# mLSTM stage: the gate products of the layer input between the two tiles' head products, and the next turn ahead of turning back

## The reference, cut to what matters

```
xm, z = split(x @ W_up)                 # 288 features each
xs    = silu(conv(xm)); q, k = xs @ Wq, xs @ Wk;  v = xm @ Wv
ig    = [q,k,v] @ Wi + bi;  fg = [q,k,v] @ Wf + bf
log_D = cumsum(log_sigmoid(fg)) differences + ig, causal
C     = (q k^T / sqrt(36)) * exp(log_D - max)
h     = (C / normalizer) @ v;  h = layernorm per head
out   = ((h + skip * xs) * silu(z)) @ W_down;  x = x + out
```

## Time and profile before

| | us |
|---|---|
| median of 3 runs | 2554.04 (2553.14 to 2554.78) |
| the profiled execution, its own time | 2551.11 |
| its span, first to last instruction | 2549.3 |
| TensorE busy | 2162.4 (85% of the span) |
| VectorE busy | 1468.7 (58%) |
| ScalarE busy | 894.0 (35%) |
| GpSimd busy | 833.8 (33%) |
| mean granted clock of TensorE | 0.879 |
| nine turns of the mLSTM stage, from the scores of turn 0 to those of turn 9 (93.85 to 353.59) | 259.74 |

### The profile page before, as it was taken

The page is one execution under the profiler, slowest core; times in us unless marked ns, Lnnn a source line. Parts: engine busy times, 40 slices in busy tenths (PEclk is TensorE's granted clock), DMA queues, the critical chain, the costliest instruction groups (busy, mean ns, idle before and its releaser), DMA issues. The chain is left out here.

```text
span 2549.3 us, 46768 instructions
## 1 busy us (share of the span) xinstructions
PE 2162.4 (85%) x17513; PEld 1876.4 (74%) x17513; DVE 1468.7 (58%) x3846; ACT 894.0 (35%) x1929; POOL 833.8 (33%) x799
## 2 busy tenths in 40 slices
PE   8999995689789857996899979998999996663598
PEld 7778873477678756995677668887999996552497
DVE  1666776656667764533999863332444336777434
ACT  0444446522244413333556531111111113676111
POOL 0111015700011063554656530330333331472446
PEclk9988995799899958997999989998999998655599
DMA  9900000090000054551000014013656652000353
GB/s 272 192 1 1 1 1 20 3 228 2 2 2 2 2 186 153 177 184 51 11 11 11 1 38 183 28 38 104 231 207 215 216 178 63 1 1 0 122 171 122
DMA packets 118115, 218.72 MB, mean 86 GB/s; under 512 B 14539, under 2 KB 90262, under 8 KB 111106
## 3 DMA queue, kind: packets, MB, share of 16 engines
q1 hardware_dynamic: 106978, 195.05, 24.8%
q0 software_dynamic: 10912, 20.67, 2.5%
HBM read 164.55 MB, written 51.11 MB: 85 GB/s over the span
## 5 line engine op out<-in xcount | busy, mean ns | idle before, releaser
L2745 ACT ACTIVATE bl_swiglu_sg<-psum 128x384 f32<-128x384 f32 x102 | 50.0, 490 | 303.5 <-PE psum L2692 303.5
L2681 PE MATMUL psum<-bl_swiglu_xt,bl_swiglu_w 128*128 128x128 f32 x1224 | 147.5, 278 | 2.2 <-DVE bl_swiglu_hid L2798 1.6
L2681 PEld LDWEIGHTS psum<-bl_swiglu_xt,bl_swiglu_w 128*128 128x128 f32 x1224 | 145.5, 195 | 3.0 <-issue 3.0
L2643 POOL COPY bl_swiglu_w<-ahead_w2swiglu_w 128x1152 f32 x51 | 58.2, 1143 | 272.5 <-PE psum L2703 213.9
L2772 DVE COPY bl_swiglu_xt<-psum 128x256 f32<-128x256 f32 x51 | 21.7, 425 | 198.1 <-PE psum L2662 198.1
L2159 POOL DMA_INDIRECT rows_in<-tower_h,tower_spots x66 | 65.1, 986 | 173.4 <-DVE tower_spots L3096 140.0
L2757 ACT ACTIVATE bl_gelu_hid<-psum,bl_gelu_w 128x128 f32<-128x128 f32 x258 | 71.1, 376 | 111.6 <-POOL bl_gelu_w L2643 108.4
L2703 PE MATMUL psum<-bl_swiglu_w,bl_swiglu_hid 128*128 128x192 f32 x612 | 107.9, 326 | 0.0
L2703 PEld LDWEIGHTS psum<-bl_swiglu_w,bl_swiglu_hid 128*128 128x128 f32 x612 | 98.3, 190 | 0.1
L3028 ACT ACTIVATE shared_sg<-psum 128x512 f32<-128x512 f32 x54 | 32.2, 597 | 187.8 <-PE psum L2965 187.8
L2958 PE MATMUL psum<-tower_xT,shared_w 128*128 128x256 f32 x432 | 96.4, 380 | 0.6 <-ACT tower_xT L3022 0.6
(11 more groups left out here) (694 smaller groups left out, 6028.2 us busy)
## 6 DMA issues: line engine op xcount, KB each, us to landing
bl_swiglu_w<-in_swiglu_w SPq DMA_DIRECT2D x51, 1152.0 KB, 5.1
bl_gelu_w<-in_gelu_w SPq DMA_DIRECT2D x43, 576.0 KB, 4.4
bl_relu_w<-in_relu_w SPq DMA_DIRECT2D x25, 576.0 KB, 4.3
rows_in<-tower_zeros SPq DMA_DIRECT2D x1, 14065.0 KB, 62.9
rows_in<-tower_zeros SPq DMA_DIRECT2D x1, 13968.0 KB, 61.0
ahead_w2swiglu_w<-in_swiglu_w SPq DMA_DIRECT2D x1, 9216.0 KB
tok_x<-in_x SPq DMA_DIRECT2D x11, 648.0 KB, 12.6
ahead_w2gelu_w<-in_gelu_w SPq DMA_DIRECT2D x1, 5400.0 KB
```

Of the source, the lines that this page charges most:

```text
L2643: pool.tensor_copy(w2[:, n % DEEP], w2all[:, e, :].rearrange("p e n -> p (e n)")).then_inc(s_w2, 1)
L2681: pe.matmul(up_tile(n, j, i, side), w[:, o:o + 128], xt[:, n % 2, side, :], start=(i == 0), stop=False, skip_group_check=True)
L2745: act.activation(sg[:, j], bank_pair(n, j)[:, 0, 0:3 * BLOCK].rearrange("p (i n) -> p i n", i=3), ACT.Silu).then_inc(s_silu, 1)
```

## The change

Three things. The two gate products of pair p + 1 (one over 128 rows, one over 64) leave `project` and become `gates_of_input`, which `attend(p)` calls behind the eight head products of the first tile. They now open the sum in bank 4 (`start`), and the first product of the queries no longer does. `p_o` is signalled by the last head product as before. In front of the turns the two are called right before `queries(0)`. And `turn(p + 2)` stands ahead of `turn_back(p)`.

```diff
                     for m in range(4):
                         for k in range(2):
                             pe.wait_ge(c_xs, MC * p + k + 1)
-                            pe.matmul(out(m), w[:, k, m * 128:(m + 1) * 128], xs[:, k, :], start=(m % 2 == 0 and k == 0), stop=False,
-                                      skip_group_check=True)
-                        if gate and m == 0:
-                            pe.matmul(out(0), wgx[:, 0, :], hT[:, p % 2, 0, :], start=False, stop=False, skip_group_check=True)
-                            pe.matmul(out(0), wgx[64:128, 1, :], hT[64:128, p % 2, 1, :], start=False, stop=False, skip_group_check=True)
+                            pe.matmul(out(m), w[:, k, m * 128:(m + 1) * 128], xs[:, k, :],
+                                      start=(m % 2 == 0 and k == 0 and not (gate and m == 0)), stop=False, skip_group_check=True)
...
+                def gates_of_input(p, k):
+                    pe.wait_ge(*((c_e, 4 * p) if p else (c_z, 2)))
+                    r = slice(64 * k, 128)
+                    pe.matmul(bank(4)[:, 0:C], wgx[r, k, :], hT[r, p % 2, k, :], start=(k == 0), stop=False, skip_group_check=True)
...
                 def attend(p):
+                    more = p + 1 < NP
...
-                    ins.then_inc(p_o, 1)
-
+                            if (u, a) == (1, 1):
+                                ins.then_inc(p_o, 1)
+                            if more and u == 0 and a == 1:
+                                gates_of_input(p + 1, 0)
+                                gates_of_input(p + 1, 1)
...
                 pe.wait_ge(s_gate, 1)
+                gates_of_input(0, 0)
+                gates_of_input(0, 1)
                 queries(0)
...
-                    turn_back(p)
                     if p + 2 < NP:
                         turn(p + 2)
+                    turn_back(p)
```

## The result

| | before | changed |
|---|---|---|
| median, us | 2551.53 (20 runs, 2539.72 to 2556.67) | 2540.26 (20 runs, 2533.34 to 2546.48) |
| ratio, with its 95% interval | | 0.9961 (0.9951 to 0.9972) |
| span of the profiled execution, us | 2549.3 | 2538.1 |
| nine turns of the stage, us | 259.74 | 246.65 |
| granted clock over these nine turns | 0.88 | 0.94 |

The change makes the kernel faster by 11.3 us in the medians. With 20 runs of each it is plain that one execution is not another: the same kernel differs by 17 us from run to run before, by 13 after. The three runs of before that were shown ahead of the forecast lay closer together (2553.14 to 2554.78) than the twenty do, and 2.5 us above their median.

A forecast was written before the change was run, and what follows sets the result against it. It took TensorE as the bound, slowed by clock falls in seven of nine mLSTM turns. 9 x 25.65 + 0.97 + 9 x 0.64 + 2 x 2.5 = 242.6 against 259.74, 17.2 us off 2554.04: 2537 us, range 2529 to 2547.

The forecast's parts named there:

- At the full clock TensorE sets the turn: In mLSTM turns without a clock fall, TensorE sets the length, with waits of only 0.4, 0.3 and 0.13 us.
- the falls as the thing to gain: Clock falls in seven of nine mLSTM turns were said to cost 27.9 us, 1.1% of the kernel.
- +0.64 us in an undisturbed turn: Cost per full-clock turn: `hn` comes 1.01 us later, partly covered by the next turn's transposes, so keys start 0.64 later.
- 1 to 3 falls in nine, for the sum 2: Clock falls expected to remain in the nine turns once the thin head products are cut, each costing 2.5 us.
- full-width products: The gate products between the head products: 1.0 us with about 4 x 0.18 us of array work, cutting the 3.4 us thin stretch.
- The later stages: Work behind the nine turns: same work 17 us earlier, nothing in the sum, about 3 us either way in the range.
- The signs: Expected in the changed profile: turns of about 26.3 us, clock 1.00 in at least six of nine, `hn` wait 0.7 to 0.8.
- Its sign of being wrong: Among the signs of failure in the nine turns: five or more still with a clock under 0.9.
- Rival A: Falls hang on the 0.4 us of idleness before `attend` and stay: 4.7 us less, 2549.3 us; chance 0.09.
- Rival B: Longer `attend` and a 0.77 us wait make nearly all turns fall: 6.5 us more, 2560.5 us; chance 0.03.
- C: Later stages fall more often or longer and take back 9 to 12 us: 2546 to 2549 us; chance 0.08.
- The thresholds without a wait: TensorE reaches the thresholds at 115.59, after `gf` at about 114.88, so they need no wait, with 0.7 us to spare.

The follow-up runs named there:

- e2: The kernel before with only the next turn moved ahead of turning back, gate products left in the queries; 2548.24 us, ratio 1.0005 to the kernel before.
- e1: The changed kernel with the next turn put back behind turning back, so only the gate products move; 2541.13 us, ratio 0.9980 to the kernel before.
- e4: The changed kernel with the second gate product over 128 rows instead of 64, zeros as new weights; 2523.24 us, ratio 0.9913 to the kernel before.
- e9: The changed kernel with the first gate product done twice in its place, the second overwriting the first; 2531.42 us, ratio 0.9928 to the kernel before.
- e10: The changed kernel itself measured once more beside the kernel before; 2540.96 us, ratio 0.9973 to the kernel before.
- e3: The changed kernel with both gate products ahead of the head products, in TensorE's 0.40 us idle gap; 2529.19 us, ratio 0.9936 to the kernel before.
- e5: The kernel before, in its own order, with only the second gate product over 128 rows; 2533.08 us, ratio 0.9938 to the kernel before.

## Why the prediction was right, and where its terms were off

The forecast was 2537 us, 17.2 under before, by fewer falls of the clock. Measured: 11.3 under by the medians, 13.1 in the stage by the profiles. The sign held, and the gain did come from falls that cost less; its size was two thirds. The time forecast, 2537, lies only 3.3 us from the median of 2540.26. Part of that is luck: the median of 20 runs of before is 2.5 us under the 2554.04 that the forecast started from.

- **"At the full clock TensorE sets the turn" and the falls as the thing to gain:** right. e2 leaves no gain for the next turn's move alone, e1 gains without it, and e4 and e9 reach a stage without a fall, 231.4 and 238.1 us.
- **+0.64 us in an undisturbed turn:** too high; it is 25.98 - 25.65 = 0.33. The term took `hn` as late by the 1.01 us that the gate products take. They took 1.10 us, but the chain from the end of the head products to `hn` got shorter: 5.30 us before (102.48 to 107.78), 4.87 after (105.02 to 109.89). Rows of GpSimd and VectorE in the first turn show why. Of the kernel before:

```profile
100.68 1.27 POOL L482 TENSOR_TENSOR ml_scale<-ml_sz,ahead_ml_nw 128x648 f32<-128x648 f32 x1 [29.60 <-ACT ml_sz L714]
101.91 1.56 POOL L484 TENSOR_TENSOR ml_shift<-ml_shift,ml_sz 128x648 f32<-128x648 f32 x1
```

```profile
102.90 0.59 DVE L864 SCALAR_TENSOR_TENSOR ml_sm<-ml_sm,ml_thr 108x16 f32<-108x16 f32 x1
```

Of the changed kernel:

```profile
103.32 1.55 POOL L484 TENSOR_TENSOR ml_shift<-ml_shift,ml_sz 128x648 f32<-128x648 f32 x1
```

```profile
105.44 0.17 DVE L872 SCALAR_TENSOR_TENSOR ml_sm<-ml_sm,ml_thr 108x16 f32<-108x16 f32 x1
...
109.13 0.76 DVE L890 TENSOR_TENSOR ml_hn<-psum,ml_sm 108x576 f32<-108x576 f32 x1
```

  Before, the small operation L864 took 0.59 us, from 102.90 to 103.49, and ended with GpSimd's L484 at 103.47. After, GpSimd is done at 104.87, before VectorE comes to the same operation (there L872) at 105.44, and it takes 0.17. All eleven of L872 take 0.17 to 0.18 us, while L864 takes 0.18 in some turns and up to 0.59 in others. The move bought 0.4 us by getting out of GpSimd's way. The Trainium skill, "SBUF — State Buffer", section "SBUF: two separate sides", has this rule: VectorE with two inputs from SBUF and GpSimd take turns at a shared pair of ports, and the later one is blocked until the other is through. The trace agrees, with 0.59 against 0.17 us. The forecast took the chain's length from the first turn without asking what in it was due to GpSimd.
- **"1 to 3 falls in nine, for the sum 2", at 2.5 us each:** this is the term that was mis-sized. Six turns had falls, one of them two, which cost 4 x 1.15 + 2.80 + 4.47 = 11.9 us instead of 5.0 (some 1.7 of it for the one behind the narrow products of the fourth turn, which the forecast did not look at). The cut by "full-width products" was counted as if both were full: the second works on half the rows. e4 and e9 show what was missing: with a little more full work no turn of their profiles falls. That the falls which stay are mostly short, with the queries in full width behind them, was not foreseen either.
- The sum of the two: 9 x (0.64 - 0.33) = 2.8 us less loss than forecast, 6.9 us more for falls; 17.2 + 2.8 - 6.9 = 13.1, as the profiles have it.
- **The later stages** were put at nothing with 3 us either way: they take 0.5 us more in these two profiles. Runs of one kernel scatter by 13 to 17 us; how much of that is theirs was not looked at.
- **The signs** that the forecast named came out mixed. It asked for a clock of 1.00 in at least six of nine turns, and three had it (five in e10); for turns of 26.3 us, and they took 25.98; for a wait of 0.7 to 0.8 us for `hn`, and it was 0.30. Its sign of being wrong, five or more turns with a clock under 0.9, did not show, but only because most falls were short: two turns were under 0.9, four at 0.94.
- **Rival A (falls stay, tied to the idle gap)** is refuted in its cause: e3 falls without the gap, e4 and e9 do not fall with it. In its count it was nearer than the forecast, since six turns still fell. The rule of the Trainium skill that was cited for it, in "TensorE: Matmul & The Clock Gate", section "Why this matters for your kernels", ties the drop to idle gaps between bursts of matmuls, and means gaps much longer than the 0.40 us here. It describes none of the falls at the head products: TensorE is recorded as busy from the start of the head products until the clock falls, in e3 without a gap ahead of them. **Rival B** (slower) and **C** (the gain given back later) did not happen.
- **"The thresholds without a wait"** held: TensorE's waits in the nine turns are the 0.40 for `cc`, the 0.3 for `xm`, and `hn` in the three undisturbed turns:

```profile
PE psum L617 <- DVE ml_cc L864: 3.6, 9, 0.4
PE psum L630 <- DVE ml_hn L890: 0.9, 3, 0.3
```

## What to carry to other kernels

Compare the length of equal turns before anything else: if they differ at the same instruction count, look at the granted clock, and find which stretch precedes each fall; a TensorE that is recorded as busy without a pause, but with narrow products, can lose its clock (e3). Then put full-width work that is due anyway between the narrow products, or let a half-filled product run over all rows with zeros. Here that cost no time (an undisturbed turn takes 25.64 us in e5 against 25.65 before, 25.60 in e4 against 25.98) and took off more than the reordering. Do not take the number of falls from one profile as the kernel's own; the length of an undisturbed turn is.

## What the runs showed that was not expected

- A product over 64 of 128 rows between products over 108 or 128 rows costs more than one over all rows: four gate instructions take 1.10 us with the second product over 64 rows, 0.82 with it over 128 (e4). Why is not shown.
- Useless work made the kernel faster: 0.37 us added to each of nine turns, 9.5 us off the time (e9 against e10).
- Full rows for one product in each turn of the kernel before gave 17.6 us, a ratio of 0.9938 (e5).
